# Transposes of the inverse's seed one slot earlier on VectorE, and another bank order for the 56 projections of a block

## The chip, the cores and the metric

The kernel runs on one core of one Trainium2 chip. A core has TensorE (PE: matmuls and weight loads), VectorE (DVE), ScalarE (ACT), GpSimd (POOL) and SyncE (SP, which here issues DMAs only). The five run their own instruction lists in order and meet at semaphores. The metric is the device time of one launch in microseconds (us), taken as the median of several runs.

## The reference, cut to what matters

The model is one layer over 8 sequences of 1024 tokens with 128 channels: gated delta attention with three inner steps per token, a layer norm, a mixture of eight small feed-forward networks, and another layer norm. Only the attention is touched.

```
q = _short_conv(x @ Wq, conv_q)           # 8 heads of 128 channels
k = _short_conv(x @ Wk, conv_k)           # 3 x 8 heads
v = _short_conv(x @ Wv, conv_v)           # 3 x 8 heads
...
y = silu(sum(xp[:, i:i + t, :] * w[:, i] for i in range(4)))     # _short_conv: four taps
...
def step(S, inp):                         # a scan over the tokens, per head
    S = S * exp(g)
    for i in range(3):
        S = S + beta_i * k_i (v_i - k_i S)
    o = q S
```

So a block of 128 tokens needs 8 + 24 + 24 = 56 projections of 128 x 128, each of which goes through four taps and a SiLU, and the scan over the tokens.

## The kernel before, in words

**Blocks and quarters.** The 8192 tokens are 64 blocks of 128 rows (`NSC`), and a block has four quarters (`CPS`, c = 0 to 3) of 32 tokens, that is 96 rows of keys. The scan is done a quarter at a time in its matrix form, which needs the inverse of a 96 x 96 triangle for each head. Four works are interleaved: the projections of block i, the preparation of a quarter of block i-1 (`prep`), the inverse of the quarter prepared one step before (`invn`), and the state update of the one before that (`run`).

**Slots.** Each quarter is written as 14 slots (`SLOTS`, k = 0 to 13), and every engine's list is written slot by slot, by hand. In slot k of quarter c TensorE issues projection m = 14c + k (L478, into a bank of `PP`), ScalarE makes the first tap from it (L692, into the ring `CY`), VectorE adds the other three taps one slot later (L780, called `tap`), and ScalarE takes the SiLU two slots after that (L769). The other work hangs on slot numbers: the eight stages of the inverse stand in slots 1, 3, 4, 6, 8, 10, 12 and 13 (`INV_AT`), as matmuls into the bank `PI` on TensorE (L493 and L495) and one operation on VectorE that takes each result out (L787, L792). Stage 0 multiplies by `XB`, the transpose of the seed `Y1`, which GpSimd builds in four operations (L986, L988) once VectorE has made `U` and `UQ` (L859, L861, slots 7 and 9). VectorE writes `XB` by a 32 x 32 block transpose (L795, `flip`), and raises `x1t_sb`, on which stage 0 waits in slot 1 of the next quarter.

**Three banks of `PP`.** Projection m goes into bank m % 3. TensorE may write it when VectorE has taken all three taps of the tile that was in the bank. For m of 2 to 55 that is the tile three before. As 56 is not a multiple of 3, the first two projections of a block (m = 0 and 1) find in their banks the tiles 54 and 55 of the block before, which are only two back; the wait at L477 is written so: `3 * (T - 1) if m < 2 else 3 * (T - 2)`. A wait for the tile two back is called a close reuse here.

**Where blocks meet.** `all_steps` (L405) writes two blocks straight out, then a loop of 31 passes (L409) whose body is two blocks (half 0 and half 1), then two draining steps. So between two blocks there are two kinds of edge: the inner edge in the middle of the body (from half 0 to half 1), and the loop edge, where every engine takes the backward branch. At the start of each block TensorE also has two 512-column matmuls (L593, L597), whose results ScalarE puts through Exp (L697, L699), with a table load before and after.

**Other names below.** L507 is the read of the old state and L834 what VectorE makes of it (`BZ`, slots 2 and 5). L519 makes rows of the keys, of which ScalarE takes sums of squares (L705). L544 and L552 stand in slot 11 of TensorE (read-out and new state of heads 0 to 3) and L801 is VectorE's addition to the state, which waits for L552. L825 are four small operations in slot 10 of quarter 3. L712 are eight sums of squares on ScalarE in slots 0 and 1 of quarter 2, for which L842 on VectorE waits in slot 2. L469 transposes the next input tile in slot 12 of quarter 3 and L918 copies it out. L903 transposes the result of stage 7.

Of the kernel before, what the change touches and what calls it, by code (L numbers as in the profile page):

```python
# [10 lines left out]
P = 128  # L11
# [4 lines left out]
HALO = TAPS - 1  # L16
# [5 lines left out]
TILES = NHEAD * (1 + 2 * NHH)  # L22
# [5 lines left out]
STEPS = 8  # L28
# [2 lines left out]
NPC = NCH * NHEAD // PIECE  # L31


STAGES = ["W0", "H", "H1", "H2", "W1", "H", "H1", "H2"]
assert len(STAGES) == STEPS

# [10 lines left out]
def need(eng, sem, value):  # L47

    if isinstance(value, int) and value <= 0:
        return  # L50
    eng.wait_ge(sem, value)
# [7 lines left out]
def over(ap, shape, axis):  # L59

    return ap.unsqueeze(axis).broadcast_to(shape)


def tile_of(m):

    nv = NHH * NHEAD
    if m < nv:
        return "v", m % NHH, m // NHH
    m -= nv
    if m < nv:  # L70
        return "k", m % NHH, m // NHH
    return "q", 0, m - nv
# [41 lines left out]
def attention_part(nc, x, Wq, Wk, Wv, Wb, Wa, A_log, dt_bias, conv_q, conv_k, conv_v, Wg, rms_weight, Wo,  # L114
                   consts, x1):
    ctx = ExitStack()
    with ctx:
# [3 lines left out]
        def pb(name, shape):  # L121
            return ctx.enter_context(nc.psum_tensor(name, shape, F32))

        def sem(name):
            return ctx.enter_context(nc.semaphore(name))
# [39 lines left out]
        with pctx:  # L165
# [23 lines left out]
            with nc.Block() as block:  # L189
# [86 lines left out]
                def _(dve):  # L276
# [24 lines left out]
                    for s, c in enumerate((13, 11, 9, 7, 5, 3)):  # L301
# [72 lines left out]
        PP = pb("PP", [P, 3, 512])  # L374
# [4 lines left out]
        inv = PI[0:R, 0:NHEAD * BK].rearrange("p (h c) -> p h c", h=NHEAD)  # L379
        join = PB[0:R, :].rearrange("p (h c) -> p h c", h=NHEAD)  # L380
        quad = PB[:, :].rearrange("p (h c) -> p h c", h=4)
        ptile = lambda m: PP[:, m % 3, 0:HALO + P]
        row_bank = lambda l, h: (PA, PK)[l][0:R, h % LH]
        lanes = [slice(0, 4), slice(4, 8)]
        heads = [range(0, 4), range(4, 8)]
# [4 lines left out]
        xt_ps, xt_sb, proj_ps, tap0_sb, taps_sb, kqv_sb = (sem(n) for n in (  # L390
            "xt_ps", "xt_sb", "proj_ps", "tap0_sb", "taps_sb", "kqv_sb"))
# [3 lines left out]
        vr_ps, vp_sb, seed_sb, y1_sb, x1t_sb, x2t_sb, x3t_sb, inv_ps, inv_sb, diag_sb, join_ps, join_sb = (  # L395
            sem(n) for n in ("vr_ps", "vp_sb", "seed_sb", "y1_sb", "x1t_sb", "x2t_sb", "x3t_sb", "inv_ps", "inv_sb",
                             "diag_sb", "join_ps", "join_sb"))
# [27 lines left out]
        def stage_bufs(k):  # L425

            base = (Y1, Y2)[k // 4]
            return {"W0": (base, None, None), "W1": (base, None, None), "H": (base, base, T0), "H1": (base, T0, T1),
                    "H2": (base, T1, (Y2, Y3)[k // 4])}[STAGES[k]]

        def when(i, c):

            n = 4 * i + c
            ahead, prep, invn, run = n, n - 4, n - 5, n - 6
            return ahead, prep, invn, run, *(known(w, 0, NCH) for w in (ahead, prep, invn, run))

        with nc.Block() as block:
# [27 lines left out]
            def _(pe):  # L465
# [5 lines left out]
                def project(i, half, m):  # L471
                    kind, hh, h = tile_of(m)
                    T = TILES * i + m
                    if m == 0:
                        pe.wait_ge(xt_sb, 2 * i + 2)
                    need(pe, taps_sb, 3 * (T - 1) if m < 2 else 3 * (T - 2))
                    w = {"q": WQ[:, h], "k": WK[:, hh * NHEAD + h], "v": WV[:, hh * NHEAD + h]}[kind]  # L477
                    pe.matmul(ptile(m), w, XT[:, half], start=True, stop=True).then_inc(proj_ps, 1)  # L478

                def invert(w, par, k):  # L480
                    if k == 0:
                        pe.wait_ge(x1t_sb, w + 1)
                    elif k == 4:
                        pe.wait_ge(x2t_sb, w + 1)
                    else:
                        pe.wait_ge(inv_sb, STEPS * w + k)
                    pe.sem_inc(begun, 1)
                    base, term, _ = stage_bufs(k)
                    for h in range(NHEAD):
                        for b in range(NBK):  # L490
                            r = slice(BK * b, BK * b + BK)
                            if STAGES[k][0] == "W":
                                mm = pe.matmul(inv[r, h], U[r, par, h, r], XB[r, h], start=True, stop=True)  # L493
                            else:
                                mm = pe.matmul(inv[r, h], WB[r, h], term[r, h], start=True, stop=True)  # L495
                    mm.then_inc(inv_ps, 1)
# [80 lines left out]
                def program(i, half, c):  # L577
# [7 lines left out]
                    for k in range(SLOTS):  # L585
                        if do_inv and k in INV_AT:
                            invert(invn, 1 - par, INV_AT[k])
                        if known(i, 0, NSC):
                            project(i, half, SLOTS * c + k)
# [185 lines left out]
            def _(dve):  # L775
# [7 lines left out]
                def inv_out(w, k):  # L783
                    dve.wait_ge(inv_ps, STEPS * w + k + 1)
                    base, _, to = stage_bufs(k)
                    if STAGES[k][0] == "W":
                        dve.tensor_tensor(WB[:, :, :], inv, over(merge[int(STAGES[k][1])], [R, NHEAD, BK], 1), ALU.mult).then_inc(inv_sb, 1)  # L787
                    else:
# [5 lines left out]
                def flip(to, of):  # L794
                    return dve.transpose(to[:, :, :].rearrange("p h c -> p (h c)"), of[:, :, :].rearrange("p h c -> p (h c)"))  # L795
# [9 lines left out]
                def group(i, half, c, k, part):  # L805

                    ahead, prep, invn, run, do_ahead, do_prep, do_inv, do_run = when(i, c)
# [72 lines left out]
                        dve.tensor_scalar(X1[:, half], YL[:, :], MV[:, 0:1], RS[:, 0:1], ALU.subtract, ALU.mult).then_inc(x1_sb, 1)  # L880
                    if k == 12 and next_x and part == 0:
                        x_in(i + 1, 1 - half)
                    if k == 13 and do_prep and part == 1:
                        dve.wait_ge(y1_sb, prep + 1)
                        flip(XB, Y1).then_inc(x1t_sb, 1)
                def program(i, half, c):
                    ahead, prep, invn, run, do_ahead, do_prep, do_inv, do_run = when(i, c)
                    rc, par = (c - 2) % 4, c % 2
                    out_now = c == 2 and known(i - 2, 0, NSC)
                    gate_now = c == 3 and known(i - 1, 0, NSC)  # L890
                    next_x = c == 3 and known(i + 1, 1, NSC)
                    for k in range(SLOTS):
                        if do_inv and k in INV_AT:
                            inv_out(invn, INV_AT[k])
                            if INV_AT[k] == 3:
                                dve.wait_ge(inv_sb, STEPS * invn + 4)
                                flip(XB, Y2).then_inc(x2t_sb, 1)
                            if INV_AT[k] == 7:
                                dve.wait_ge(inv_sb, STEPS * invn + 8)
                                need(dve, join_ps, 3 * (invn - 1) + 1)  # L900
                                for b in range(2):
                                    r = slice(BK * b, BK * b + BK)
                                    op = dve.transpose(X3[r, :, r], Y3[r, :, :])  # L903
                                op.then_inc(x3t_sb, 1)
                        j, jh, m = lagged(i, half, SLOTS * c + k - 1)
                        taps = known(j, 0, NSC)
                        if taps:
                            tap(j, m, 1)
                        group(i, half, c, k, 0)
                        if taps:  # L910
                            tap(j, m, 2)
                        group(i, half, c, k, 1)
                        if taps:
                            tap(j, m, 3)

                def x_in(i, half):
                    dve.wait_ge(xt_ps, i + 1)
                    dve.tensor_copy(XT[:, half, HALO:], PB[:, 0:P]).then_inc(xt_sb, 1)  # L918
                    dve.tensor_scalar(XT[:, half, 0:HALO], XT[:, 1 - half, P:], C[:, bass.ds(C_KEEP + i % NSC, 1)],
                                      None, ALU.mult).then_inc(xt_sb, 1)  # L920
# [501 lines left out]
```

## Time and profile before

| | us |
|---|---|
| median of 3 runs | 8919.44 (8914.47 to 8927.09) |
| the profiled execution, its own time | 8925.8 |
| its span | 8924.0 |

| engine | busy us | share of the span |
|---|---|---|
| PE | 7944.6 | 89% |
| PE weight loads | 6671.9 | 75% |
| DVE | 6744.4 | 76% |
| ACT | 5415.4 | 61% |
| POOL | 3168.8 | 36% |

The span is the time between the first and the last instruction of the program; 1.8 us lie around it. A row of a timeline gives the start in us from the beginning of the span, the time to the end of the last of its instructions, the engine, the line of the kernel, the operation, the tile written and the tiles read, shapes and the number of instructions; in brackets the idle time of that engine before the first of them and what ended it. A projection is two matmul instructions (x2), four heads are x4 or x8. PEclk is the granted clock of TensorE as a share of full speed: 1.00 is 2.4 GHz, 0.50 is 1.2 GHz. "issue" means that no other engine is seen to have ended the idle time. The attention is the first 7.75 ms, the feed-forward part the rest.

### The profile page before, as it was taken

What the parts mean: (1) busy time and instruction counts of PE and PEld (TensorE: products, weight loads), DVE (VectorE), ACT (ScalarE), POOL (GpSimd) and SP (SyncE); (2) the same over time, 40 slices, a digit from 0 to 9 for tenths busy, and PEclk for the clock granted to TensorE, in tenths of its full rate; (3) what the DMA queues carried; (4) which work ended last, traced back from release to release, by engine and by line L of the source; (5) the groups of instructions that cost most, each with busy time, mean ns of one, the idle gap of its engine ahead of it and who ended that gap; (6) DMA issues with size and microseconds to landing.
All of it is one profiled execution on the core that took longest, in us unless ns stands there. A gap on an engine that the chain in (4) does not pass through costs nothing. (4 is left out here: it accounts for less than half of the span.)

```text
span 8924.0 us, 423618 instructions
## 1 busy us (share of the span) xinstructions
PE 7944.6 (89%) x156132; PEld 6671.9 (75%) x156132; DVE 6744.4 (76%) x22809; ACT 5415.4 (61%) x19287; POOL 3168.8 (36%) x5052
## 2 busy tenths in 40 slices
PE   3888989898889888989889898989898988979999
PEld 2677777777777777777777777777777777767777
DVE  5888888888888888888888888888888888733333
ACT  2666666666666666666666666666666666623333
POOL 0333334443433334443334343443334434411111
PEclk6899999999999999999999999999999999889999
DMA  1000000000000000000000000000000000010000
GB/s 44 4 5 6 6 6 6 6 5 6 5 6 6 6 6 6 6 5 6 6 6 6 6 5 6 5 6 6 6 6 6 6 6 5 5 28 8 9 10 8
DMA packets 72477, 64.75 MB, mean 7 GB/s; under 512 B 16944, under 2 KB 67392, under 8 KB 69952
## 3 DMA queue, kind: packets, MB, share of 16 engines
q1 hardware_dynamic: 70208, 35.32, 1.4%
q8 instruction: 1323, 21.68, 1.1%
q14 instruction: 946, 7.75, 0.3%
HBM read 26.92 MB, written 8.39 MB: 4 GB/s over the span
## 5 line engine op out<-in xcount | busy, mean ns | idle before, releaser
L780 DVE SCALAR_TENSOR_TENSOR CY<-PP,CWV,CY 128x128 f32<-128x128 f32 x4608 | 1587.9, 345 | 109.0 <-DVE CY L780 6.3
L780 DVE SCALAR_TENSOR_TENSOR CY<-PP,CWK,CY 128x128 f32<-128x128 f32 x4608 | 1585.5, 344 | 77.0
L986 POOL TENSOR_TENSOR Y<-U,C 32x256 f32<-32x256 f32 x768 | 554.5, 722 | 1223.9 <-DVE UQ L861 1183.8
L478 PE MATMUL PP<-XT,WV 128*128 128x131 f32 x3072 | 781.7, 343 | 221.6 <-issue 118.3
L692 ACT ACTIVATE CY<-PP,CWK 128x128 f32<-128x128 f32 x1536 | 562.9, 366 | 543.0 <-PE PP L478 535.0
L954 POOL TENSOR_TENSOR YF<-Y,ones 32x256 f32<-32x256 f32 x768 | 551.5, 718 | 784.0 <-DVE Y L792 743.9
L495 PE MATMUL PI<-T,WB 32*32 32x32 f32 x49152 | 722.8, 192 | 120.1 <-DVE T L792 118.9
L478 PE MATMUL PP<-XT,WK 128*128 128x131 f32 x3072 | 768.8, 338 | 68.2 <-DVE CY L780 68.2
L705 ACT ACTIVATE EM<-PK 128x128 f32<-128x128 f32 x2048 | 538.6, 280 | 474.5 <-PE PK L519 474.4
L495 PEld LDWEIGHTS PI<-T,WB 32*32 32x32 f32 x49152 | 610.5, 107 | 272.2 <-issue 202.4
L692 ACT ACTIVATE CY<-PP,CWV 128x128 f32<-128x128 f32 x1536 | 560.1, 365 | 395.5 <-PE PP L478 388.4
L493 PEld LDWEIGHTS PI<-XB,U 32*32 32x32 f32 x24576 | 353.2, 118 | 534.6 <-issue 497.7
L769 ACT ACTIVATE KQ<-CY 128x128 f32<-128x128 f32 x2048 | 740.4, 362 | 8.3
L478 PEld LDWEIGHTS PP<-XT,WV 128*128 128x128 f32 x3072 | 503.6, 208 | 315.6 <-issue 129.7
L493 PE MATMUL PI<-XB,U 32*32 32x32 f32 x24576 | 407.9, 204 | 367.8 <-DVE XB L795 367.8
L1197 ACT ACTIVATE HS<-PH,B1S 128x512 f32<-128x512 f32 x512 | 352.7, 689 | 610.0 <-PE PH L1116 610.0
L801 DVE SCALAR_TENSOR_TENSOR S<-S,WHOLE,PK 128x128 f32<-128x128 f32 x2048 | 613.4, 342 | 141.5 <-PE PK L552 141.4
L507 PE MATMUL PA<-S,KQ 128*128 128x128 f32 x4096 | 702.2, 328 | 0.0
L1125 PEld LDWEIGHTS PY<-W2S,HS 128*128 128x128 f32 x4096 | 533.9, 192 | 217.9 <-issue 214.8
L834 DVE SCALAR_TENSOR_TENSOR BZ<-PA,HEADD,VP 128x128 f32<-128x128 f32 x2048 | 618.2, 345 | 82.3 <-PE PA L507 52.8
L507 PEld LDWEIGHTS PA<-S,KQ 128*128 128x128 f32 x4096 | 656.9, 243 | 0.7 <-issue 0.2
L966 POOL TENSOR_TENSOR S<-R,BETA 96x4 f32<-96x4 f32 x512 | 101.9, 199 | 1519.3 <-DVE R L821 1519.3
(231 smaller groups left out, 19750.7 us busy)
## 6 DMA issues: line engine op xcount, KB each, us to landing
XR<-in_L_attn_x SPq DMA_DIRECT2D x65, 64.0 KB, 1.9
XL<-in_L_attn_x SPq DMA_DIRECT2D x16, 256.0 KB, 2.8
XRES<-in_L_attn_x SPq DMA_DIRECT2D x64, 64.0 KB, 1.9
x<-X SPq DMA_DIRECT2D x64, 64.0 KB, 2.0
XI<-x SPq DMA_DIRECT2D x16, 256.0 KB, 3.1
out<-OUT SPq DMA_DIRECT2D x16, 256.0 KB, 2.3
W1S<-in_L_ffn_W SPq DMA_DIRECT2D x1, 2048.0 KB
WK<-in_L_attn_Wk SPq DMA_DIRECT2D x1, 1536.0 KB, 10.2
```

The costliest lines, as they stand in the source:

```text
L478: pe.matmul(ptile(m), w, XT[:, half], start=True, stop=True).then_inc(proj_ps, 1)
L493: mm = pe.matmul(inv[r, h], U[r, par, h, r], XB[r, h], start=True, stop=True)
L495: mm = pe.matmul(inv[r, h], WB[r, h], term[r, h], start=True, stop=True)
L507: mm = pe.matmul(PA[:, h % LH], KQ[:, rs, h, rc], S[:, h], start=True, stop=True)
L692: act.activation(CY[:, m % RING], ptile(m)[:, 0:P], ACT.Copy, scale=taps_of(m)[:, 0:1]).then_inc(tap0_sb, 1)
L705: op = act.activation(EM[:, h], PK[:, h], ACT.Square, accum_out=SSR[:, c, h:h + 1])
L769: act.activation(to, CY[:, m % RING].rearrange("p (c t) -> p c t", c=CPS), ACT.Silu).then_inc(kqv_sb, 1)
L780: dve.scalar_tensor_tensor(CY[:, m % RING], ptile(m)[:, s:s + P], taps_of(m)[:, s:s + 1], CY[:, m % RING], ALU.mult, ALU.add).then_inc(tap ...
L801: op = dve.scalar_tensor_tensor(S[:, h], S[:, h], WHOLE[:, run, h:h + 1], PK[:, h], ALU.mult, ALU.add)
L834: op = dve.scalar_tensor_tensor(BZ[:, h], PA[:, h % LH], HEADD[:, run, h:h + 1], VP[:, par, h], ALU.mult, ALU.add)
L954: pool.tensor_tensor(YF[r, :, r], Y3[r, :, :], over(ones[r, 0:BK], [BK, NHEAD, BK], 1), ALU.mult).then_inc(diag_sb, 1)
L986: pool.tensor_tensor(Y1[r, :, :], U[r, par, :, r], over(first[r, :], [BK, NHEAD, BK], 1), ALU.mult).then_inc(seed_sb, 1)
```

## The change

Three places are edited. The seed's transpose (`flip(XB, Y1)`) moves from the second half of VectorE's slot 13 to the second half of slot 12, in every quarter; it still waits for `y1_sb`. Stage 0 of the inverse gets one more wait on TensorE, for `inv_sb` at `STEPS * w`, the end of stage 7 of the inverse before, since the transpose now stands ahead of that operation in VectorE's list and no longer implies it. And the bank of a projection comes from a table in place of m % 3: it turns 0, 1, 2 up to m = 18, from m = 19 on 0, 2, 1, and from m = 53 on forward again, so that after m = 55 in bank 2 the next block's m = 0 and 1 find tiles 53 and 54. The two close reuses are then m = 19 (slot 5 of quarter 1) and m = 53 (slot 11 of quarter 3).

```diff
+PBANK, CLOSE = [0, 1], (19, 53)
+for _m in range(2, TILES):
+    PBANK.append(PBANK[_m - 2] if _m in CLOSE else 3 - PBANK[_m - 1] - PBANK[_m - 2])
...
-        ptile = lambda m: PP[:, m % 3, 0:HALO + P]
+        ptile = lambda m: PP[:, PBANK[m], 0:HALO + P]
...
-                    need(pe, taps_sb, 3 * (T - 1) if m < 2 else 3 * (T - 2))
+                    need(pe, taps_sb, 3 * (T - 1) if m in CLOSE else 3 * (T - 2))
...
                     if k == 0:
+                        need(pe, inv_sb, STEPS * w)
                         pe.wait_ge(x1t_sb, w + 1)
...
-                    if k == 13 and do_prep and part == 1:
+                    if k == 12 and do_prep and part == 1:
                         dve.wait_ge(y1_sb, prep + 1)
                         flip(XB, Y1).then_inc(x1t_sb, 1)
```

VectorE's list at the end of quarter 3, ahead of the inner edge, before (L780 are the taps of tiles 53 and 54, L792 takes out stage 7, L903 transposes it, L795 is the seed's transpose, L51 holds waits):

```order
L51 REGISTER_ALU [waits diag_sb]
L792 TENSOR_TENSOR Y<-Y,PI 96x256 [waits join_ps]
L51 REGISTER_ALU [waits inv_sb]
L903 STREAM_TRANSPOSE X<-Y 32x8x32 [waits join_ps]
L903 STREAM_TRANSPOSE X<-Y 32x8x32
L778 REGISTER_ALU
L51 REGISTER_ALU [waits tap0_sb]
L780 SCALAR_TENSOR_TENSOR CY<-PP,CWQ,CY 128x128 [waits taps_sb]
L51 REGISTER_ALU [waits tap0_sb]
L780 SCALAR_TENSOR_TENSOR CY<-PP,CWQ,CY 128x128 [waits taps_sb]
L795 STREAM_TRANSPOSE XB<-Y 96x256 [waits y1_sb]
L51 REGISTER_ALU [waits tap0_sb]
```

The same place now (line numbers are 4 or 5 higher: L785 are the taps, L797 stage 7, L908 its transposes, L800 the seed's transpose):

```order
L800 STREAM_TRANSPOSE XB<-Y 96x256 [waits y1_sb]
L55 REGISTER_ALU [waits tap0_sb]
L785 SCALAR_TENSOR_TENSOR CY<-PP,CWQ,CY 128x128 [waits taps_sb]
L789 REGISTER_ALU
L55 REGISTER_ALU [waits inv_ps]
L55 REGISTER_ALU [waits diag_sb]
L797 TENSOR_TENSOR Y<-Y,PI 96x256 [waits join_ps]
L55 REGISTER_ALU [waits inv_sb]
L908 STREAM_TRANSPOSE X<-Y 32x8x32 [waits join_ps]
L908 STREAM_TRANSPOSE X<-Y 32x8x32
L783 REGISTER_ALU
L55 REGISTER_ALU [waits tap0_sb]
```

The transpose stood behind the second tap of tile 54; it now stands ahead of the third tap of tile 53 (the L785 right behind it) and ahead of stage 7.

TensorE's list across the inner edge, before (L478 is the projection m = 0 of the new block, L493 stage 0 of the inverse):

```order
L478 MATMUL PP<-XT,WV 128x131 [waits taps_sb]
L51 ISA [waits xt_sb,gsil_sb]
L593 MATMUL PB<-GM,C 96x512 [waits gm_sb,join_sb]
L51 ISA
L51 ISA [waits s_sb]
L597 MATMUL PK<-GM,C 96x512 [waits vp_sb,u_sb]
L493 MATMUL PI<-XB,U 32x32 [waits x1t_sb]
L493 MATMUL PI<-XB,U 32x32 x23
```

And now (L482 the projection, L498 stage 0):

```order
L482 MATMUL PP<-XT,WV 128x131 [waits taps_sb]
L55 ISA [waits xt_sb,gsil_sb]
L598 MATMUL PB<-GM,C 96x512 [waits gm_sb,join_sb]
L55 ISA
L55 ISA [waits s_sb]
L602 MATMUL PK<-GM,C 96x512 [waits vp_sb,u_sb]
L55 ISA
L498 MATMUL PI<-XB,U 32x32 [waits inv_sb,x1t_sb]
L498 MATMUL PI<-XB,U 32x32 x23
```

No matmul moves on TensorE. Stage 0 has a second wait, and the value of the wait on `taps_sb`, which the list doesn't print, is one tile older at m = 0 and 1 and one tile younger at m = 19 and 53.

## Rows read from the trace of the kernel before

**Rows 1.** Stretches: busy time of each engine, then PEclk, DMA share, GB/s.
```profile
1000.00:7000.00 6000.00, 5388.35 (x118084) 4638.51 (x118075) 4966.04 (x16802) 3932.16 (x14683) 2395.50 (x3922) 0.92 0.02 5
4013.97:4020.80 6.83, 6.18 (x94) 5.91 (x95) 5.99 (x22) 1.97 (x11) 1.33 (x2) 0.50 0.11 31
4044.70:4054.93 10.23, 10.23 (x100) 6.99 (x101) 5.12 (x18) 6.30 (x17) 0.61 (x1) 0.50 0.01 2
4102.72:4106.14 3.42, 3.42 (x25) 3.40 (x16) 3.31 (x13) 0.87 (x4) 0.33 (x1) 0.50 0.03 7
```

**Rows 2.** Waits of 1000 to 7000 us: total, times, longest.
```profile
PE PI L493 <- DVE XB L795: 290.3, 151, 2.1
PE PP L478 <- issue: 97.3, 25, 4.4
```

**Rows 3.** The loop's branch on TensorE's sequencer: ns min/median/max.
```profile
L409 PEldq COMPARE_BRANCH  x31: 83/4414/5074, 580.2 to 7741.5; - x31
```

**Rows 4.** Timeline, all engines, an inner edge, in order of time.
```profile
4043.20 0.31 ACT L769 ACTIVATE KQ<-CY 128x128 f32<-128x128 f32 x1
...
4044.52 0.67 PE L478 MATMUL PP<-XT,WV 128*128 128x131 f32 x2 [2.37 <-DVE CY L780]
...
4045.31 0.37 ACT L692 ACTIVATE CY<-PP,CWV 128x128 f32<-128x128 f32 x1 [1.79 <-PE PP L478]
...
4049.90 0.42 DVE L787 TENSOR_TENSOR WB<-PI,C 96x256 f32<-96x256 f32 x1 [3.46 <-PE PI L493]
...
4055.95 0.42 DVE L792 TENSOR_TENSOR T<-Y,PI 96x256 f32<-96x256 f32 x1 [1.76 <-PE PI L495]
...
4056.30 0.31 ACT L769 ACTIVATE KQ<-CY 128x128 f32<-128x128 f32 x1
...
4056.66 0.66 PE L519 MATMUL PK<-C,KQ 128*128 128x128 f32 x4 [0.35 <-ACT KQ L769]
...
4058.01 0.42 DVE L792 TENSOR_TENSOR T<-Y,PI 96x256 f32<-96x256 f32 x1 [0.32 <-PE PI L495]
```

**Rows 5.** Busy time in a stretch of that edge (columns of rows 1).
```profile
4045.31:4056.61 11.30, 11.00 (x150) 7.66 (x150) 5.17 (x19) 7.57 (x20) 0.61 (x1) 0.57 0.02 4
```

**Rows 6.** Timeline, start of a quarter 1.
```profile
4076.24 0.69 DVE L780 SCALAR_TENSOR_TENSOR CY<-PP,CWV,CY 128x128 f32<-128x128 f32 x2
4076.45 0.70 PE L493 MATMUL PI<-XB,U 32*32 32x32 f32 x48 [1.85 <-DVE XB L795]
...
4077.08 0.49 PE L478 MATMUL PP<-XT,WV 128*128 128x131 f32 x2
```

**Rows 7.** Timeline, slot 2 of quarter 2 in two following blocks.
```profile
3989.12 0.17 DVE L842 TENSOR_SCALAR FA<-QSE 128x8 f32<-128x8 f32 x1 [0.54 <-ACT OGT L712]
...
4108.48 0.17 DVE L842 TENSOR_SCALAR FA<-QSE 128x8 f32<-128x8 f32 x1 [2.09 <-ACT OGT L712]
```

**Rows 8.** Timeline of VectorE and of TensorE, start of a quarter 3.
```profile
4014.40 0.69 DVE L780 SCALAR_TENSOR_TENSOR CY<-PP,CWK,CY 128x128 f32<-128x128 f32 x2
...
4021.80 0.42 DVE L792 TENSOR_TENSOR T<-Y,PI 96x256 f32<-96x256 f32 x1 [1.74 <-PE PI L495]
...
4014.62 1.07 PE L493 MATMUL PI<-XB,U 32*32 32x32 f32 x48 [2.07 <-DVE XB L795]
4015.62 0.81 PE L478 MATMUL PP<-XT,WK 128*128 128x131 f32 x2
```

**Rows 9.** Timeline of TensorE and of VectorE, slots 11 and 12 of quarter 3.
```profile
4036.02 0.49 PE L478 MATMUL PP<-XT,WQ 128*128 128x131 f32 x2
...
4040.39 0.27 PE L469 MATMUL PB<-C,XR 128*128 128x128 f32 x1
...
4036.84 1.12 DVE L780 SCALAR_TENSOR_TENSOR CY<-PP,CWQ,CY 128x128 f32<-128x128 f32 x3
4038.31 0.60 DVE L801 SCALAR_TENSOR_TENSOR S<-S,WHOLE,PK 128x128 f32<-128x128 f32 x2 [0.35 <-PE PK L552]
```

**Rows 10.** Timeline of GpSimd: the end of the seed in a quarter 3.
```profile
4036.68 0.72 POOL L988 TENSOR_TENSOR Y<-Y,C 96x256 f32<-96x256 f32 x1
```

More of the change, by code:

```diff
@@ L31 @@
 NPC = NCH * NHEAD // PIECE
+PBANK, CLOSE = [0, 1], (19, 53)
+for _m in range(2, TILES):
+    PBANK.append(PBANK[_m - 2] if _m in CLOSE else 3 - PBANK[_m - 1] - PBANK[_m - 2])
+assert len({PBANK[-2], PBANK[-1], PBANK[0]}) == 3 and PBANK[1] not in (PBANK[-1], PBANK[0])
 STAGES = ["W0", "H", "H1", "H2", "W1", "H", "H1", "H2"]
```

## The prediction

> **What bounds the kernel now.** I read the engines' shares first, then the granted clock by stretches, the list of waits, and last the timelines around the joints between quarters. TensorE is busy 89% of the span and VectorE 76%, and neither is the bound alone: from 1000 to 7000 us VectorE works 4966 of 6000 us and TensorE's granted clock is 0.92, so part of its business is the same work at 1.2 GHz [rows 1]. The two hold each other at the joints. TensorE waited 151 times, 290.3 us in all, for the seed's transpose, which is 1.92 us at the start of quarters 1, 2 and 3 [rows 2]. At a block's start it has another wait. On an inner edge projection m = 0 stood 2.37 us for VectorE's taps of tile 54; then TensorE ran at 0.50 for 10.23 us, and VectorE stood 3.46 us for stage 0 and 1.76 us for stage 1 [rows 1, 4]. On a loop edge the same projection waited 97.3 / 25 = 3.9 us for "issue" [rows 2], and the branch of TensorE's sequencer took 4.4 us at the median [rows 3]: there it isn't the taps that hold it.
>
> **The close reuse at m = 0, inner edge.** With the wait one tile older, m = 0 needs tile 53. In VectorE's list that tile ends ahead of stage 7 and its transposes, before TensorE is free, which is 2.37 us ahead of 4044.52. TensorE goes on at full clock, the seed's transpose has been made, and stage 0 runs while VectorE is in slot 0, so VectorE's 3.46 us go. What is late next is ScalarE. From the first tap of m = 0 to the SiLU of tile 55, at whose end the second L519 starts, ScalarE works 7.57 us in 11.30 [rows 5], two table loads among it; in the new order it finds each input there. It can begin at 4043.20 + 0.31 = 4043.51 and ends at 4051.1, where today it ends at 4056.61. L519 and then stage 2 follow it as today, 4058.01 - 4056.61 = 1.40 us to VectorE's L792: 4052.5 in place of 4058.01, 5.5 us earlier [rows 4]. VectorE itself would be there at 4058.01 - 0.32 - 1.76 - 3.46 = 4052.5 or before, so it doesn't hold it up. From both sides: if the clock stays low none the less, only TensorE's 2.37 us come back. I take 5.5, as every input of ScalarE's chain is ready by rows. About 32 inner edges.
>
> **The loop edge.** The branch stays, so I count 0 here. The Trainium skill says in "Advanced Engine Details and Errata", Control Flow Timing, that a compare-and-branch takes about 108 ns. By that rule the 3.9 us would be something the change can remove. The row says 4414 ns at the median, forty times that, and the row decides [rows 3]. The rule's outcome is the second rival below.
>
> **The earlier transpose, quarters 1, 2 and 3.** The work on VectorE is the same; it moves ahead of the third tap of tile 14c - 3, which it delays by 0.4 us, and everything from the end of slot 13 is where it was. GpSimd has the seed ready at 4036.68 + 0.72 = 4037.4 [rows 10], and the transpose will stand in slot 12, behind the L801 that starts at 4038.31 [rows 9], so the wait moved with it costs nothing; GpSimd starts the seed on slot 9's `UQ` in every quarter, so the margin is much the same in the others. The added wait on `inv_sb` is met by VectorE's first operation of slot 13, when TensorE is no further than m = 14c: 0, or a tenth of a us of sequencer work hidden behind matmuls. Stage 0 then no longer stands for the transpose, but the next projection, m = 14c + 1, stands for the third tap of tile 14c - 2, the last of slot 13. In a quarter 1 that tap ends at 4076.24 + 0.34 = 4076.58, where the projection today starts at 4077.08 [rows 6]. So of a stall of 1.85 us only 0.5 us come back to TensorE; the rest turns into a wait on taps. What it is worth depends on who waits behind it:
> - Quarter 1: VectorE waits for nothing there at full clock. 0 to 0.2, I take 0.1.
> - Quarter 2: VectorE waits 0.54 us for ScalarE's sums of squares at full clock and 2.09 us where TensorE was at 0.50 [rows 1, 7]. ScalarE's chain starts from the projection and L519, both 0.5 us earlier. So 0.5 us in every block, and up to 1.3 (the mean of 0.54 and 2.09) if the low stretches go too. I take 0.9.
> - Quarter 3: the tap ends at 4014.40 + 0.34 = 4014.74 and the projection started at 4015.62, so TensorE gains 0.9 us even at the low clock of this stretch [rows 1, 8]. VectorE waits 1.74 us for stage 1, which is all there is to get at full clock. Here over half of TensorE's 2.07 us of idle time stays, as a wait for that tap, and with it perhaps the low clock, so I take 1.2, between 0.9 and 1.7; 0 if another wait steps in.
>
> **The two new close reuses.** At m = 19 TensorE must see the end of VectorE's slot 4 before it writes in slot 5. Nobody waits for that projection until VectorE's slot 6, and the next stage of the inverse depends on slot 4 as well: 0. At m = 53 it must see tile 51 done, in slot 10 of quarter 3, which has the four L825 ahead of two of its taps. That last tap starts at 4036.84 + (1.12 - 0.34) / 2 = 4037.2 and ends near 4037.6; TensorE today writes at 4036.02 [rows 9]. So it will stand 1.6 us. Behind it in TensorE's list are the read-out and the new state, and VectorE in slot 11 already waits 0.35 us for that: L801 starts 2.29 us after the projection, now at 4039.9 in place of 4038.31. There is no slack: 1.6 us lost in each block. At worst the idle time also drops the clock: from 4038.31 to the end of L469 at 4040.66 TensorE has 2.3 us of work that VectorE waits for, which would double, 3.9 in all. Stalls of 1.85 us at full clock are survived sometimes and sometimes not, so I put a tenth of that on top: 1.8.
>
> **The sum.** For two blocks, with one inner edge: 5.5 + 2 x (0.1 + 0.9 + 1.2 - 1.8) = 6.3 us. For 32 pairs, 202 us. The profiled execution took 8925.8 us, so 8724; the median of the runs shown is 6.4 us below it, so I forecast **8717 us**, 2.3% less. With the bounds of the terms alone the pair gives 5.5 + 2 x (0.2 + 1.3 + 1.7 - 1.6) = 8.7 (8641 us) at best and 2.4 + 2 x (0 + 0.5 + 0 - 3.9) = -4.4 (9060 us) at worst.
>
> **The rivals.**
> 1. *Small gain: the clock stays low.* The new waits on taps at the starts of the quarters are cut up but still there, and an inner edge follows a quarter with 1.6 us of new idle time. Then the inner edge gives 2.4, quarter 2 gives 0.5 and quarter 3 0.9: 2.4 + 2 x (0.5 + 0.9 - 1.6) = 2.0, 64 us, 8855. For it: 2.07 us of idle time was enough for the low stretch of rows 1. Against it: at the inner edge none is left.
> 2. *The loop edge gains too.* If the 3.9 us are the taps after all, the pair gives 6.3 + 3.9 = 10.2, 326 us: 8593. Against it stand the row of the branch and the name "issue".
> 3. *The clock pays more.* If TensorE alone bounded the kernel, each low stretch would give back half its length: 5.1 + 2.4 at the inner edge, 3.4 in quarter 3, 1.7 in one of quarters 1 and 2: 7.5 + 2 x (3.4 + 1.7 - 1.6) = 14.5, 464 us, 8455. Against it: in the low stretch at quarter 3 VectorE is busy 5.99 of 6.83 us [rows 1]. The Trainium skill reckons that way ("TensorE: Matmul & The Clock Gate", HAM oscillation: the cost of low clock is its duration times the share of pulses withheld), which by this trace holds only where nobody else is due.
> 4. *Slower: the projection m = 53.* If the 1.6 us of idle time in slot 11 drop the clock in every block, the price there is 3.9 us twice in a pair, 7.8. It decides once the rest gives less than 7.8: with 2.4 from the inner edge and 0.5 from each quarter 2 the pair loses 4.4, 141 us, 9060.
> 5. *No difference.* The waits only change names: m = 53 costs 3.2 in a pair and the rest gives as much, since quarters 2 and 3 find another late engine. 8919.
>
> **How the numbers follow.** Forecast 0.66, rival 1 0.12, rival 2 0.05, rival 3 0.03, rival 4 0.08, rival 5 0.06. The forecast's own range is 8650 to 8800. The range that should hold 8 times in 10 takes in the small gain: 8640 to 8860. A change of 0.2% (18 us) is about what a measurement of this kernel can tell from none: faster than that 0.86, within it 0.06, slower 0.08.
>
> **What would show it.** Right: on inner edges m = 0 without a wait, no 3.46 us ahead of stage 0's L787, and the granted clock at 1.00 there; on loop edges 3.9 us as now; the waits for the seed's transpose gone and in their place waits of m = 14c + 1 for taps, about 1.3 us each; the projection m = 53 idle for 1.6 us, and VectorE's L801 of quarter 3 waiting 1.9 us and not 0.35. Wrong: a low granted clock behind m = 53, the inner edge still at 0.50, or VectorE waiting at the transpose for GpSimd.

## The result, and the profile after

The changed kernel takes 8694.3 us (median of 4 runs, 8682.6 to 8712.5), the one before 8917.0 us beside it. The ratio is 0.9751, with a 95% interval of 0.9732 to 0.9771: 2.5% faster, 23 us under the forecast and inside its range. Its profiled execution took 8692.4 us with a span of 8690.6 us, and TensorE's mean granted clock rose from 0.913 to 0.944.

The waits of the changed kernel from 1000 to 7000 us (who waited at which line for whom: total, times, longest; line numbers are 4 or 5 higher than before):

```profile
PE PP L482 <- DVE CY L785: 328.4, 330, 2.5
DVE S L806 <- PE PK L557: 208.0, 208, 3.6
PE PP L482 <- issue: 86.5, 23, 4.4
DVE T L797 <- PE PI L500: 68.8, 152, 1.9
DVE WB L792 <- PE PI L498: 54.7, 26, 2.9
```

TensorE's wait for the seed's transpose, 290.3 us in [rows 2], is gone from the list. In its place stand 328.4 us for taps, which are shorter each; before, the same line had 104.6 us:

```profile
PE PP L478 <- DVE CY L780: 104.6, 134, 2.4
```

Of the 328.4 us some 80 are m = 53. VectorE's wait for the new state (L806) is 1.00 us in the mean.

The branch of TensorE's sequencer, and projection m = 0 at a loop edge with the stretch behind it (columns as in [rows 3], a timeline, and [rows 1]):

```profile
L413 PEldq COMPARE_BRANCH  x31: 83/4262/4885, 574.4 to 7522.7; - x31
```
```profile
4275.02 0.80 PE L482 MATMUL PP<-XT,WV 128*128 128x131 f32 x2 [4.40 <-issue]
```
```profile
1000.00:7000.00 6000.00, 5398.27 (x121799) 4615.21 (x121800) 5109.85 (x17313) 4051.67 (x15119) 2465.85 (x4041) 0.95 0.02 6
4275.02:4285.00 9.98, 9.97 (x90) 6.73 (x91) 5.30 (x18) 5.88 (x16) 0.61 (x1) 0.50 0.02 4
4159.50:4172.00 12.50, 12.15 (x234) 9.51 (x232) 11.02 (x37) 10.83 (x38) 4.81 (x9) 0.86 0.01 3
```

The branch is what it was in [rows 3], and the projection still waits for it, whatever the bank order. Behind it the clock is at 0.50. The last row is the stretch behind an inner edge: 0.86, where a stretch of the same place was at 0.50 in [rows 1]. It is not the 1.00 of the prediction; in its parts:

```profile
4159.50:4163.01 3.51, 3.51 (x59) 1.80 (x58) 3.19 (x10) 3.47 (x9) 2.44 (x4) 1.00 0.02 5
4163.01:4166.43 3.42, 3.42 (x29) 3.18 (x29) 3.09 (x12) 3.32 (x12) 0.32 (x1) 0.50 0.00 0
4166.43:4172.00 5.57, 5.22 (x155) 4.53 (x151) 4.74 (x18) 4.05 (x20) 2.05 (x5) 1.00 0.01 3
```

TensorE was busy for all of the 3.51 us before the clock fell. Why it fell there, the runs don't show.

An inner edge of the changed kernel, all engines, in order of time:

```profile
4153.51 0.49 PE L482 MATMUL PP<-XT,WQ 128*128 128x131 f32 x2 [1.55 <-DVE CY L785]
...
4155.80 0.60 DVE L806 SCALAR_TENSOR_TENSOR S<-S,WHOLE,PK 128x128 f32<-128x128 f32 x2 [1.96 <-PE PK L557]
...
4159.50 0.49 PE L482 MATMUL PP<-XT,WV 128*128 128x131 f32 x2
...
4160.69 0.31 ACT L774 ACTIVATE KQ<-CY 128x128 f32<-128x128 f32 x1
4160.89 0.37 ACT L697 ACTIVATE CY<-PP,CWV 128x128 f32<-128x128 f32 x1
...
4164.01 0.41 DVE L792 TENSOR_TENSOR WB<-PI,C 96x256 f32<-96x256 f32 x1
...
4168.63 0.66 PE L524 MATMUL PK<-C,KQ 128*128 128x128 f32 x4 [0.35 <-ACT KQ L774]
...
4169.97 0.42 DVE L797 TENSOR_TENSOR T<-Y,PI 96x256 f32<-96x256 f32 x1 [0.31 <-PE PI L500]
```

The first two rows are the new close reuse, m = 53: TensorE stands 1.55 us and VectorE 1.96 us behind it, 1.6 more than the 0.35 of [rows 9]. Then m = 0 goes without a wait, and so does the first result of the inverse (L792), which stood 3.46 us in [rows 4]. ScalarE now goes from one SiLU (4160.69) straight to the first tap of the new block. From that SiLU to VectorE's take-out of stage 2 (the last row) it is 9.28 us; in [rows 4] the same two rows are 4058.01 - 4043.20 = 14.81 us apart. The difference is 5.53 us.

The starts of quarters 2 and 3 (all engines):

```profile
4102.46 0.49 PE L482 MATMUL PP<-XT,WK 128*128 128x131 f32 x2 [1.16 <-DVE CY L785]
...
4106.64 0.17 DVE L847 TENSOR_SCALAR FA<-QSE 128x8 f32<-128x8 f32 x1
```
```profile
4130.31 0.70 PE L498 MATMUL PI<-XB,U 32*32 32x32 f32 x48
4132.28 0.81 PE L482 MATMUL PP<-XT,WK 128*128 128x131 f32 x2 [1.27 <-DVE CY L785]
```

Stage 0 (L498) goes at once, and the projection behind it waits for taps, 1.16 to 1.27 us, as the prediction had it. VectorE's L847, which waited 0.54 or 2.09 us in [rows 7], waits for nothing. The low clock behind such a wait is rarer (0.95 against 0.92 in the mean from 1000 to 7000 us), but not gone; this is the stretch right behind the 1.27 us:

```profile
4132.29:4135.71 3.42, 3.42 (x16) 3.42 (x16) 3.35 (x13) 0.39 (x2) 0.78 (x2) 0.50 0.01 2
```

**Where the time went.** The table gives VectorE's pace over a pair of blocks: the time between the starts of its first tap of tile m = 14c + 4, which stands in its slot 5 (for one stretch of m = 52, in slot 11 of quarter 3), means over 27 pairs in us, even block / odd block, worked out from the starts of L780 or L785. The two rows above the sum are the two kinds of edge.

| stretch | before | changed | e1_flip | e2_banks | e3_19_47 |
|---|---|---|---|---|---|
| quarter 0 to 1 | 26.25 / 25.45 | 25.62 / 25.88 | 25.62 / 25.25 | 26.17 / 26.64 | 25.62 / 27.79 |
| quarter 1 to 2 | 26.36 / 28.03 | 25.57 / 25.83 | 25.57 / 25.84 | 26.66 / 27.51 | 25.58 / 25.84 |
| quarter 2 to 3 | 31.24 / 31.10 | 29.57 / 30.12 | 29.55 / 30.05 | 30.78 / 30.37 | 29.56 / 29.47 |
| quarter 3, slot 5 to 11 | 12.69 / 12.69 | 12.65 / 12.56 | 12.60 / 12.65 | 12.68 / 12.69 | 12.63 / 12.61 |
| slot 11 to 5, inner edge | 21.81 | 18.49 | 21.06 | 19.02 | 16.61 |
| slot 11 to 5, loop edge | 23.02 | 25.26 | 23.21 | 24.68 | 23.03 |
| sum | 238.64 | 231.55 | 231.40 | 237.20 | 228.74 |

The change took 7.1 us off a pair, where 6.3 were forecast. Quarter 2 gave 3.0, quarter 3 gave 2.7, the inner edge 3.3 net of its m = 53, and the loop edge lost 2.2 to its own m = 53.

### The profile page after: what moved, and what is told of

The parts are those of the page before. It is cut to its first block and busy times, and to the rows that moved or that the text cites. A ratio compares the mean times of both kernels' runs of the same rounds, so it can differ in the third digit from the quotient of the medians.

```text
span 8690.6 us, 423742 instructions
## 1 busy us (share of the span) xinstructions
PE 7749.3 (89%) x156132; PEld 6468.5 (74%) x156132; DVE 6732.3 (77%) x22809; ACT 5412.8 (62%) x19287; POOL 3167.6 (36%) x5052
## 5 line engine op out<-in xcount | busy, mean ns | idle before, releaser
L785 DVE SCALAR_TENSOR_TENSOR CY<-PP,CWV,CY 128x128 f32<-128x128 f32 x4608 | 1587.0, 344 | 111.5 <-ACT CY L697 13.9
L785 DVE SCALAR_TENSOR_TENSOR CY<-PP,CWK,CY 128x128 f32<-128x128 f32 x4608 | 1584.3, 344 | 77.0
L482 PE MATMUL PP<-XT,WK 128*128 128x131 f32 x3072 | 746.5, 329 | 240.9 <-DVE CY L785 230.2
L482 PE MATMUL PP<-XT,WV 128*128 128x131 f32 x3072 | 763.5, 336 | 214.2 <-DVE CY L785 102.6
L806 DVE SCALAR_TENSOR_TENSOR S<-S,WHOLE,PK 128x128 f32<-128x128 f32 x2048 | 612.5, 341 | 266.7 <-PE PK L557 266.5
L482 PEld LDWEIGHTS PP<-XT,WK 128*128 128x128 f32 x3072 | 471.1, 195 | 359.8 <-DVE CY L785 319.5
L482 PEld LDWEIGHTS PP<-XT,WV 128*128 128x128 f32 x3072 | 483.7, 200 | 327.7 <-DVE CY L785 167.6
L512 PE MATMUL PA<-S,KQ 128*128 128x128 f32 x4096 | 615.9, 300 | 1.2 <-DVE BZ L839 1.2
L785 DVE SCALAR_TENSOR_TENSOR CY<-PP,CWQ,CY 128x128 f32<-128x128 f32 x1536 | 528.3, 344 | 111.1 <-ACT CY L697 51.2
L557 PE MATMUL PK<-BZ,KD 96*128 96x128 f32 x4096 | 591.3, 289 | 0.0
```

The lines of the kernel that those rows point to most:

```text
L512: mm = pe.matmul(PA[:, h % LH], KQ[:, rs, h, rc], S[:, h], start=True, stop=True)
L557: mm = pe.matmul(PK[:, h], KD[:, rc, h], BZ[0:R, h], start=True, stop=True)
L785: dve.scalar_tensor_tensor(CY[:, m % RING], ptile(m)[:, s:s + P], taps_of(m)[:, s:s + 1], CY[:, m % RING], ALU.mult, ALU.add).then_inc(tap ...
L806: op = dve.scalar_tensor_tensor(S[:, h], S[:, h], WHOLE[:, run, h:h + 1], PK[:, h], ALU.mult, ALU.add)
```

## The experiments

Each ratio is to the kernel before, run beside it.

**1. The transpose alone, and the banks alone.** `e1_flip` is the changed kernel with the old banks, `e2_banks` the changed kernel with the old transpose.

```diff
e1_flip:
-        ptile = lambda m: PP[:, PBANK[m], 0:HALO + P]
+        ptile = lambda m: PP[:, m % 3, 0:HALO + P]
...
-                    need(pe, taps_sb, 3 * (T - 1) if m in CLOSE else 3 * (T - 2))
+                    need(pe, taps_sb, 3 * (T - 1) if m < 2 else 3 * (T - 2))
e2_banks:
-                    if k == 12 and do_prep and part == 1:
+                    if k == 13 and do_prep and part == 1:
```

> The earlier transpose alone, with the old order of banks (close reuses m = 0 and 1). Theory (the terms of the prediction are separate and each sits at its own joint): the quarters 2 and 3 keep their gain (in the trace of the changed kernel 1.3 to 1.7 us per quarter 2 and 3, some 5.6 us per pair of blocks) and nothing is lost at m = 53; the inner edge keeps its wait for the taps of tile 54. 32 x 5.6 = 180 us less than before, about 8740, ratio 0.980. Rival (the gain is the inner edge's alone, and the gains in quarters 2 and 3 come from a granted clock that the rest of the change keeps up): at most 2 us per pair, 64 us, ratio 0.993 or above.

Measured: 8661.9 us, ratio 0.9708 (0.9691 to 0.9724).

> The order of banks alone, with the transpose back in slot 13. Theory: on the inner edge m = 0 no longer waits for tile 54, but stage 0 still needs the seed's transpose, which ends 0.3 us before tile 54 does; TensorE can do its two 512-column matmuls before that, so most of the 5.5 us stay (4 to 5.5 per pair); m = 53 costs 2.2 us in each block, 4.5 per pair; quarters 2 and 3 as before. So 0 to 1 us per pair gained: 8890 to 8920, ratio 0.997 to 1.000. Rival (the close reuse at m = 53 costs nothing that was not there before, the 2.2 us are the low clock of the loop edge): ratio 0.980 to 0.985.

Measured: 8882.2 us, ratio 0.9950 (0.9927 to 0.9973).

`e1_flip` beat its own theory (0.980), and it beats the changed kernel: 0.9708 against 0.9751, with intervals that don't touch (up to 0.9724, from 0.9732). Its pair is 231.40 us, 7.2 less than before, all of it without the bank order. Its waits from 1000 to 7000 us:

```profile
PE PP L482 <- DVE CY L785: 310.0, 307, 2.6
DVE WB L792 <- PE PI L498: 146.2, 52, 3.6
DVE S L806 <- PE PK L557: 107.9, 208, 1.0
```

VectorE's wait for stage 0 behind both kinds of edge is what it was before. `e2_banks` gained 1.4 us in a pair, and 0.5% by its ratio, a little more than its theory. Two lines of the kernel before, and the waits of `e2_banks`:

```profile
DVE WB L787 <- PE PI L493: 148.0, 50, 3.6
DVE S L801 <- PE PK L552: 103.2, 201, 0.6
```

```profile
PE PI L498 <- DVE XB L800: 292.5, 152, 2.1
DVE S L806 <- PE PK L557: 196.2, 202, 3.5
DVE WB L792 <- PE PI L498: 64.6, 26, 2.8
DVE FA L847 <- ACT OGT L717: 62.2, 51, 2.1
```

The transpose is waited for as before, and so is ScalarE at L847; the wait for stage 0 at inner edges is gone (148.0 to 64.6 us, 50 times to 26), and the wait for the new state has doubled (103.2 to 196.2 us). So the bank order removes one wait and makes another of about the same size, and the gain of the change is the transpose's.

**2. The second close reuse elsewhere.** `PBANK, CLOSE = [0, 1], (19, 53)` becomes (19, 47) in `e3_19_47` and (5, 33) in `e4_5_33`.

> The changed kernel with the second close reuse at m = 47 (slot 5 of quarter 3) in place of m = 53 (slot 11 of quarter 3). In the trace before, TensorE reaches m = 47 only 0.2 us after tile 45 is done, so it should wait for nothing there. Theory (m = 53 costs 2.2 us in each block because VectorE's slot 10 is long): the 2.2 us come back in all 64 blocks, 140 us less than the changed kernel, about 8555, ratio to before 0.959. Rival (those 2.2 us move elsewhere, to VectorE's wait for the new state in slot 11 or to the loop edge, where the branch holds TensorE anyway): half of it or less, ratio 0.967 or above.

Measured: 8590.0 us, ratio 0.9628 (0.9612 to 0.9644).

> As e3_19_47, with the two close reuses in slot 5 of quarters 0 and 2 (m = 5 and 33), where TensorE arrives 0.35 and 0.03 us after the tile two back is done. Theory: slot 5 is free of cost in any quarter, so within 0.2% of e3_19_47, ratio 0.959. Rival (m = 33 has no margin, and quarter 2 is the longest): 0.2 us or more per block slower than e3_19_47.

Measured: 8629.5 us, ratio 0.9677 (0.9661 to 0.9693).

`e3_19_47` lies between its theory (0.959) and its rival (0.967). At (19, 47) the price of m = 53 is gone at both edges (table: 18.49 to 16.61, 25.26 to 23.03), and the wait for the new state is back to 0.51 us in the mean. Half of that is given back in quarter 0 of the odd block, 25.88 to 27.79. What is left makes the bank order worth 0.8% on top of the transpose (0.9708 to 0.9628). What stands there, in a timeline of all engines, and the stretches around it:

```profile
4115.20 0.95 PE L524 MATMUL PK<-C,KQ 128*128 128x128 f32 x4 [1.70 <-ACT KQ L774]
```
```profile
4106.31:4115.43 9.12, 7.42 (x156) 5.26 (x155) 8.35 (x29) 8.96 (x27) 2.77 (x4) 1.00 0.01 4
4115.43:4118.84 3.41, 3.41 (x60) 3.02 (x59) 2.20 (x8) 1.90 (x11) 2.05 (x5) 0.50 0.00 0
```

ScalarE is busy 8.96 of 9.12 us behind the inner edge: it is the late engine there, as the prediction said. TensorE waits 1.7 us for its SiLU, and only then its clock falls. `e4_5_33` missed its theory: it is 0.5% slower than (19, 47), 40 us or 0.6 us per block, so the time is on the side of its rival (0.2 us or more). That m = 33 is the cause isn't shown: no stretch of its table is more than 0.4 us longer, and the longest of these is quarter 0 to 1 of the odd block (28.18 us against 27.79), not quarter 2.

**3. Fewer loop edges.** `e5_four` is `e3_19_47` with

```diff
-            for i in range(2):
+            for i in range(4):
                 for c in range(CPS):
-                    program(i, i, c)
-            with eng.Fori(1, NSC // 2) as t:
-                for half in range(2):
+                    program(i, i % 2, c)
+            with eng.Fori(1, NSC // 4) as t:
+                for j in range(4):
                     for c in range(CPS):
-                        program(2 * t + half, half, c)
+                        program(4 * t + j, j % 2, c)
```

> As e3_19_47, but four blocks are written straight out and the loop body has four blocks, so 15 loop edges in place of 31; the work is the same. Theory (on a loop edge the sequencer's branch holds TensorE some 3.9 us, whatever the order of banks): each loop edge that becomes an inner edge saves what separates the two kinds in e3_19_47, 23.0 - 16.6 = 6.4 us from slot 11 to slot 5, less the 2.2 us that a block behind an inner edge gives back in quarter 0: about 4.2 x 16 = 67 us less than e3_19_47, ratio to before about 0.955. Rival (the wait is the taps of tile 54, or fetching the instructions of a body twice as long costs as much as the branches saved): no gain, ratio 0.963 or above.

Measured: 8530.6 us, ratio 0.9564 (0.9535 to 0.9592). 59 us less for 16 loop edges, 3.7 us each, where the theory said 4.2.

**4. TensorE's wait in quarter 0 filled.** `e6_rows_later` is `e3_19_47` with

```diff
+                        if k == 4 and c == 0 and do_prep:
+                            rows_k(1, i, c, sc, prep, run)
                         if k in (1, 4) and do_run:
                             old_state(k // 4, run, rs, rc)
-                        if k in (1, 3) and do_prep:
+                        if k in (1, 3) and do_prep and (k, c) != (3, 0):
                             rows_k(k // 2, i, c, sc, prep, run)
```

`e7_both` has this and the loop of `e5_four`; `e8_rows_53` has this and the close reuses 19 and 53.

> As e3_19_47, but in quarter 0 TensorE issues the second half of the rows of the keys (L524, which waits for ScalarE's SiLU of tile 55) in slot 4 behind stage 2 and projection 4, in place of slot 3. Theory (behind an inner edge TensorE stands 1.46 us at that matmul, its clock falls to 0.50 in slots 3 to 7 of half of the odd blocks' quarter 0, and this is where 2 us of the inner edge's gain are given back): the wait at L524 goes or falls below 0.5 us, quarter 0 of odd blocks shrinks from 27.8 to 25.5 us between the two slots 5, VectorE's 0.83 us at stage 2 go too: 3 us per pair, about 95 us less, ratio 0.952. Rival (ScalarE is the bound there, so its chain and not TensorE's idle time sets quarter 0): same as e3_19_47 within 0.2%, as the squares start no earlier.

Measured: 8569.7 us, ratio 0.9599 (0.9583 to 0.9615).

> e5_four and e6_rows_later together. Theory: their places differ and the gains add, with more inner edges to gain at (48 in place of 32): about 67 + 95 + 30 us less than e3_19_47, ratio 0.942. Rival: the one takes the other's place, ratio 0.952 or above.

Measured: 8494.9 us, ratio 0.9514 (0.9496 to 0.9532).

> e6_rows_later with the changed kernel's close reuses, m = 19 and 53. Theory (the projection m = 53 costs 1.9 to 2.2 us in every block, and only the knock-on in quarter 0 hid part of it between the changed kernel and e3_19_47): 4.1 us per pair, 130 us, more than e6_rows_later. Rival (the stall at m = 53 is partly hidden, as the 104 us between the changed kernel and e3_19_47 say): 100 us or less more than e6_rows_later.

Measured: 8697.8 us, ratio 0.9743 (0.9716 to 0.9770).

`e6_rows_later` gained 0.3% where 1.1% was expected, and its interval overlaps that of `e3_19_47`. Two of its waits, and the same two of `e3_19_47` behind them:

```profile
DVE CY L787 <- ACT CY L699: 108.0, 97, 3.2
DVE T L799 <- PE PI L500: 54.2, 99, 1.8
```
```profile
DVE CY L785 <- ACT CY L697: 56.3, 46, 3.3
DVE T L797 <- PE PI L500: 85.2, 159, 1.9
```

VectorE's wait for the later stages of the inverse fell from 85.2 to 54.2 us in the 6 ms, but its wait for ScalarE's first tap rose from 56.3 to 108.0 us. The new part stands at the tap of tile 4 in quarter 0, behind the squares that were pushed later in ScalarE's list. Measured as in the table, quarter 0 of the odd block did shrink, from 27.79 to 26.01 us, most of the way to the 25.5 of the theory; but the inner edge grew from 16.61 to 17.12 and quarter 2 to 3 by 0.3 us in each block, and why these grew wasn't tried. So removing TensorE's idle time at that matmul gave most of what it should in its own place, and the greater part of that was lost again elsewhere. `e7_both` reached 0.9514 instead of 0.942: the part of `e6_rows_later` is what is missing. `e8_rows_53` settles the price of m = 53: 0.9743 - 0.9599 = 1.44%, 128 us or 2.0 us per block, with 4.1 us per pair (131 us) expected. Between these two kernels quarter 0 of the odd block hides only 0.5 us of it per pair (25.55 and 26.01), and between the changed kernel and `e3_19_47`, 104 us apart, it hid 1.9.

**5. Why m = 53 is dear.** `e9_l825_slot11` is the changed kernel with `if k == 10 and c == 3` of VectorE's L825 made `if k == 11 and c == 3`.

> The changed kernel (close reuses m = 19 and 53) with one edit: the four small operations of L825 on VectorE stand in slot 11 of quarter 3, ahead of the state's addition, and not in slot 10. The work is the same. Theory (m = 53 costs 1.9 to 2.2 us because VectorE's slot 10 is 1.4 us longer than others): TensorE's wait at m = 53 falls from 1.55 to about 0.2 us, and L825 fills the time in which VectorE waits for the new state (2.25 us), which falls to below 0.4. About 2.2 us per block come back, less 2 us per pair in quarter 0 of odd blocks as in e3_19_47: 80 to 110 us less than the changed kernel, ratio to before 0.963 to 0.966. Rival (a close reuse is bad in any slot in which TensorE's list has the read-out and new state behind it): the wait moves with it and the time stays within 0.3% of the changed kernel.

Measured: 8589.6 us, ratio 0.9620 (0.9589 to 0.9651). Its waits:

```profile
PE PP L482 <- DVE CY L785: 245.2, 279, 1.3
DVE S L806 <- PE PK L557: 128.7, 210, 1.0
```

With the long slot shortened, the same close reuse costs little: TensorE's wait at m = 53 is 0.14 us in place of 1.55 (worked out from the starts, mean of 50 blocks), 208.0 us of waiting for the new state became 128.7, the longest 1.0 and not 3.6, and 1.3% of the time came off, as much as by moving the reuse to m = 47 (0.9620 and 0.9628). It isn't slot 11 of TensorE that was wrong, but VectorE's slot 10 ahead of it.

**6. The best of it.** `e10_best` is `e7_both` with L825 in slot 11; `e11_twelve` and `e12_thirty` have loop bodies of 12 and 30 blocks in place of 4.

> e7_both (close reuses m = 19 and 47, rows of the keys later in quarter 0, loop body of four blocks) with L825 in slot 11 too. Theory: L825 now fills VectorE's wait for the new state in quarter 3, 0.34 us per block: 15 to 25 us less than e7_both, ratio 0.949. Rival (that wait follows VectorE's own pace, as TensorE only gets there as VectorE frees banks): no difference.

Measured: 8511.4 us, ratio 0.9539 (0.9522 to 0.9555). No gain over `e7_both` (0.9514), and rather a loss, with intervals that overlap: the rival.

> e10_best with a loop body of twelve blocks, 5 passes, so 10 fewer loop edges. Theory (a loop edge costs some 4 us more than an inner edge, from e5_four: 59 us for 16): 37 us less than e10_best, ratio 0.945. Rival (a body of that length has its own cost in fetching instructions, which grew with the body already in e5_four): no gain or a loss.

Measured: 8377.3 us, ratio 0.9389 (0.9361 to 0.9417).

> e11_twelve with a loop body of thirty blocks in 2 passes, so 3 fewer loop edges (2 in place of 5, the last of each followed by the draining steps). Theory (a loop edge costs 13 us with what follows it: in e10_best the block at the loop edge and the three behind it are 12.8 us longer than the steady 109.3 us of a block): 8377 - 3 x 13 = 8338 us, ratio to before 0.935. Rival (the branch's own 4 us only, and the steady 109.3 us of e11_twelve come from a fortunate state of the clock that a longer stretch loses again): 12 us less or slower.

Measured: 8354.5 us, ratio 0.9369 (0.9352 to 0.9386).

Ten fewer loop edges took off 134 us where the theory of `e11_twelve` had 37: 13 us each, three times the branch. A loop edge of `e10_best`, the two blocks before and behind it, and nine steady blocks of `e11_twelve` and the one across its loop edge:

```profile
4179.61 0.80 PE L482 MATMUL PP<-XT,WV 128*128 128x131 f32 x2 [4.13 <-issue]
4180.62 0.35 DVE L787 SCALAR_TENSOR_TENSOR CY<-PP,CWQ,CY 128x128 f32<-128x128 f32 x1 [2.83 <-issue]
```
```profile
4066.00:4179.60 113.60, 99.83 (x2350) 85.44 (x2349) 100.31 (x340) 79.18 (x298) 49.69 (x81) 1.00 0.02 6
4179.60:4295.90 116.30, 108.12 (x2350) 92.26 (x2350) 96.51 (x329) 76.95 (x287) 45.37 (x75) 0.91 0.02 5
```
```profile
3459.50:4443.60 984.10, 896.11 (x21143) 768.08 (x21142) 882.46 (x3007) 700.77 (x2629) 427.77 (x702) 1.00 0.02 6
4443.60:4557.00 113.40, 101.34 (x2352) 86.87 (x2350) 100.17 (x340) 79.39 (x298) 49.67 (x81) 0.98 0.02 6
```

Nine blocks in 984.1 us are 109.3 us each at full clock. A loop edge makes the block that ends with it 4 us longer, and the block behind it 7 us longer at a clock of 0.91. That an edge saved only 3.7 us from `e3_19_47` to `e5_four` fits this. Per pass, and measured as in the table, the body of two blocks took 10 us more than two steady ones, the body of four 16 us more (`e5_four`; 15 in `e10_best`), the body of twelve 20 us more. In a short body the next edge comes before the effect of the last has died out, so going from two to four blocks removes less per edge than going from four to twelve. `e12_thirty` gave 23 us for three edges fewer, between its theory (39) and its rival (12), with intervals that overlap; blocks of 113 us turn up in it far from any loop edge, and why wasn't tried. It is the fastest version, 6.3% under the kernel before.

## Why the prediction was right

**What bounds the kernel.** Right: the two engines hold each other at the joints, and the main terms sat where the prediction put them. What it gave nothing for and the table shows is 0.8 us per pair at the inner edge from the transpose alone (21.81 to 21.06).

**The inner edge.** The mechanism and its size were right, 5.5 forecast and 5.53 between matching rows of one edge; over all pairs the edge is 21.81 - 16.61 = 5.2 us shorter where m = 53 doesn't stand in it (`e3_19_47`). The granted clock of 1.00 that the prediction wanted there was 0.86, so "TensorE goes on at full clock" was not quite so. And what the sum missed is that the gain isn't all the bank order's to keep. With the transpose already moved, the banks are worth 21.06 - 18.49 = 2.6 us at this edge with m = 53 in it, and 4.5 without, of which quarter 0 of the odd block takes back 0.6 (changed) or 2.5 (`e3_19_47`). The forecast named ScalarE as the late engine and left out that TensorE then stands at L524, behind which the clock fell in the rows above.

**The loop edge.** Right: 4.40 us of "issue" in the row above, a branch of 4.26 us at the median, and `e5_four` got 3.7 us for each one removed. The rival that took the wait for taps is out, as the bank order that relaxes it left the wait standing. The Trainium skill's 108 ns ("Advanced Engine Details and Errata", Control Flow Timing) is not what TensorE's branch takes in this kernel.

**The earlier transpose.** The mechanism was right in each part (1.85 us of waiting turned into 1.2 us for taps, no wait for GpSimd, L847 free), but the term was too small: 4.4 us per pair forecast, 7.2 measured by `e1_flip`. Of the difference, quarter 2 has 1.2 (3.0 per pair and not 1.8, which is more than the bound of 1.3 a block), the inner edge 0.8, quarter 1 0.6 (0.8 and not 0.2) and quarter 3 0.3. The bound for quarter 2 counted what VectorE stood at L842; that the rest is what the low stretches cost the slots behind it is likely, but no run separates it. That the lower clock went too is seen at `e1_flip`'s 0.95 from 1000 to 7000 us against 0.92 in [rows 1].

**The close reuses.** m = 19 cost nothing that could be seen. For m = 53 the 1.6 us at full clock were right to 0.01 (VectorE's 1.96 - 0.35); the mean is nearer 2.0 (1.88 and 2.23 in the table, 2.0 by `e8_rows_53`), forecast 1.8. The clock makes the difference: in 14 of 52 blocks it was low behind m = 53, and there VectorE's wait was 3.0 us in the mean and up to 3.6, against 1.96 in the other 38. This is the sign of being wrong that the prediction named, met in a quarter of the blocks. One of them:

```profile
4383.47 0.49 PE L482 MATMUL PP<-XT,WQ 128*128 128x131 f32 x2 [1.55 <-DVE CY L785]
4386.33 0.60 DVE L806 SCALAR_TENSOR_TENSOR S<-S,WHOLE,PK 128x128 f32<-128x128 f32 x2 [2.53 <-PE PK L557]
```
```profile
4384.88:4391.70 6.82, 6.82 (x119) 6.10 (x117) 3.19 (x13) 1.84 (x8) 0.00 (x0) 0.50 0.00 0
```

**The sum.** 6.3 forecast, 7.1 measured per pair, but that it came so near is partly luck, by errors that cancel: the transpose gave 2.8 more than forecast, and the bank order, put at 5.5 - 3.6 = 1.9, gave about nothing (231.40 to 231.55) and by the measured times cost 0.4%.

**The rivals.** By its time the second (8593) is the nearest, and its mechanism is out. The first had part of the mechanism: short waits for taps stay at the starts of the quarters, and behind some of them the clock still falls, but not often enough to hold the gain to 64 us. The fourth's low clock behind m = 53 came in 14 of 52 blocks and not in every one. The third, that low clock pays back half its length, can be set against the mean clocks. They make 2 x (1 - 0.913) x 8924 = 1553 us at low clock before and 2 x (1 - 0.944) x 8690.6 = 973 after. By the Trainium skill's reckoning ("TensorE: Matmul & The Clock Gate", HAM oscillation) the 580 us less would be worth 290, an estimate; the kernel gained 223, part of it from waits that had nothing to do with the clock. So here the reckoning overstates. A reason that fits is that VectorE was due anyway, busy 5.99 of 6.83 and 3.31 of 3.42 us in two low stretches of [rows 1].

## What to carry to other kernels

A wait for a buffer moved to another place costs what the releasing engine's slot ahead of that place is long: look for where the waiting engine already arrives later than the release (0.1 to 0.2 us late at m = 19 and 47, 1.57 us early at m = 53), and not for where the waiting engine's own slot is light. Being late by itself isn't proof: `e4_5_33`, with arrivals 0.35 and 0.03 us late, came out 0.5% behind `e3_19_47`. When two edits are made at once, time each alone; here the bank order, which the sum gave 5.5 us and took 3.6 from, was worth nothing with the m = 53 it came with. Before tuning the order inside a loop, count what its backward edge costs with all that follows it.

## What the runs showed of the hardware that was not expected

A backward branch held TensorE's sequencer 3.8 to 4.7 us at the median in every kernel here with five passes or more, and 83 ns on the last pass, where the loop is left. The same branch on VectorE took 63 ns, yet VectorE's first tap behind it in `e10_best` came after 2.83 us of "issue". What the sequencers do in that time isn't shown. The cost to the kernel was 13 us per edge from `e10_best` to `e11_twelve`, as the block behind the edge ran at a clock of 0.91, and less where the body was shorter or far longer (3.7 us from two blocks to four, 8 us from twelve to thirty). TensorE fell to 1.2 GHz behind idle times of 1.27 to 2.4 us, also once with none in the 3.51 us before (at 4163.01 in the changed kernel), and stayed at 2.4 GHz behind others of 1.85 us at the start of a quarter 1 [rows 6]. So the same wait can cost nothing in one block and 1.7 us in the next, as from quarter 1 to 2 before (26.36 and 28.03 us in the table).
